# C-weighted sums of a selective scan: two of four sequences moved from VectorE to ScalarE and GpSimd

## What is computed

```python
dt = softplus(ts @ W_dt.T + b_dt)              # 2048 channels
def step(state, inp):                          # over the 128 tokens of a sequence
    dt_t, B_t, C_t, u_t = inp
    dA = exp(dt_t[..., None] * A)              # A: 2048 channels x 16 states
    state = state * dA + (dt_t * u_t)[..., None] * B_t[:, None, :]
    y = einsum('bdn,bn->bd', state, C_t)       # sum over the 16 states, weighted by C
y = (ys + x * D) * silu(gate);  out = y @ W_out.T
```

## Time and profile before

| what | value |
|---|---|
| median of three runs | 3445.48 us |
| span of the profiled execution, first to last instruction | 3444.0 us |
| PE busy | 2894.4 us (84%) |
| DVE busy | 2815.9 us (82%) |
| ACT busy | 1403.2 us (41%) |
| POOL busy | 1399.2 us (41%) |
| first to last `dtu` (15 steps of the scan phase) | 558.7 to 2506.9 us |

### The profile page before, as it was taken

The page is one execution under the profiler, slowest core; times in us unless marked ns, Lnnn a source line. Parts: engine busy times, 40 slices in busy tenths (PEclk is TensorE's granted clock), DMA queues, the critical chain, the costliest instruction groups (busy, mean ns, idle before and its releaser), DMA issues.

```text
span 3444.0 us, 37416 instructions
## 1 busy us (share of the span) xinstructions
PE 2894.4 (84%) x10992; PEld 1521.9 (44%) x10992; DVE 2815.9 (82%) x3919; ACT 1403.2 (41%) x2166; POOL 1399.2 (41%) x455
## 2 busy tenths in 40 slices
PE   7999996877887877887877887877877999999996
PEld 3445453444443434444434444434443455555553
DVE  2333336999999999999999999999998677777775
ACT  1111113534434534534534534534532455555553
POOL 0000004555565565565555665555662122222221
PEclk9999997999999999999999999999999999999998
DMA  4111114120113120113120113120112121111110
GB/s 145 55 55 38 54 49 116 57 110 7 56 62 80 55 104 7 62 50 87 62 100 11 62 50 86 61 89 22 61 37 62 42 75 61 61 61 55 55 61 25
DMA packets 57906, 210.48 MB, mean 61 GB/s; under 512 B 4481, under 2 KB 4609, under 8 KB 52961
## 3 DMA queue, kind: packets, MB, share of 16 engines
q1 hardware_dynamic: 57762, 208.76, 18.2%
HBM read 172.96 MB, written 35.78 MB: 61 GB/s over the span
## 4 chain that ended last, share of the span: by engine, by line
PE 35%; DVE 34%; issue 20%; POOL 4%; ACT 4%; DVEq 2%; DMA 1%; SPq 0%; POOLq 0%; ACTq 0%
DVE arena L662 16%; PE banks L1004 13%; DVE arena L678 10%; PE banks L407 3%; PE banks L450 3%; PE banks L363 2%; PE banks L388 2%; POOL arena L1138 2%; POOL arena L1144 2%; PE banks L418 2%; DVE rbuf L687 2%; PE banks L289 1%; PE banks L378 1%; PE banks L986 1%; DVE arena L745 1%
## 5 line engine op out<-in xcount | busy, mean ns | idle before, releaser
L1144 POOL TENSOR_TENSOR arena<-arena 128x2048 f32<-128x2048 f32 x256 | 1156.9, 4528 | 620.4 <-PE banks L306 618.2
L662 DVE TENSOR_TENSOR_SCAN arena<-banks,arena 128x512 f32<-128x512 f32 x1024 | 1189.3, 1201 | 36.2 <-POOL arena L1144 19.8
L522 ACT ACTIVATE banks<-arena,a_sb 128x508 f32<-128x508 f32 x1024 | 700.1, 687 | 1151.6 <-DVE arena L662 1151.4
L306 PE MATMUL banks<-ident,arena 128*128 128x128 f32 x4096 | 665.2, 292 | 385.5 <-DVE arena L678 350.4
L306 PEld LDWEIGHTS banks<-ident,arena 128*128 128x128 f32 x4096 | 460.7, 146 | 871.7 <-DVE arena L678 712.8
L678 DVE SCALAR_TENSOR_TENSOR arena<-banks,cg,arena 128x512 f32<-128x512 f32 x960 | 664.1, 731 | 1.3 <-PE banks L306 1.0
L289 PE MATMUL banks<-arena 128*128 128x512 f32 x1088 | 523.6, 606 | 5.4 <-issue 5.4
L321 PE MATMUL banks<-arena 128*128 128x512 f32 x1024 | 501.4, 614 | 0.0
L1004 PE MATMUL banks<-arena 128*128 128x512 f32 x1024 | 444.5, 595 | 24.6 <-DMA dsk<-in_D 24.6
L1197 DVE SCALAR_TENSOR_TENSOR arena<-banks,arena 128x508 f32<-128x508 f32 (+2 forms) x192 | 142.6, 742 | 330.8 <-ACT arena L1070 326.3
L1138 POOL TENSOR_TENSOR arena<-arena 128x2048 f32<-128x2048 f32 x16 | 72.4, 4526 | 711.8 <-DMA arena<-u_scratch 551.5
(11 more groups left out here) (131 smaller groups left out, 2481.0 us busy)
## 6 DMA issues: line engine op xcount, KB each, us to landing
arena<-in_WoutT SPq DMA_DIRECT2D x17, 2048.0 KB, 8.0
arena<-in_WinZ SPq DMA_DIRECT2D x64, 512.0 KB, 3.4
arena<-in_xT SPq DMA_DIRECT2D x8, 2048.0 KB, 15.3
u_scratch<-arena SPq DMA_DIRECT2D x16, 1024.0 KB, 5.9
arena<-b_scratch SPq DMA_DIRECT2D x16, 1024.0 KB, 19.9
arena<-u_scratch SPq DMA_DIRECT2D x16, 1024.0 KB, 10.0
arena<-x_scratch SPq DMA_DIRECT2D x32, 512.0 KB, 3.5
x_scratch<-rbuf SPq DMA_DIRECT2D x5, 2048.0 KB, 7.5
```

The lines of the kernel that those rows point to most:

```text
L306: last = nc.tensor.transpose(bank(2 + b % 2)[:, i * P:(i + 1) * P], hb[n % 4][:, i * GT + b * P:i * GT + (b + 1) * P], ident[:, :])
L522: nc.scalar.activation(by_seq(bank(i % 2))[:, :, 1:SEQ], by_seq(dt[q % 2][:, i, :])[:, :, 1:SEQ], ACT.Exp, scale=a_sb[:, QD * q + i, n:n + ...
L662: nc.vector.tensor_tensor_scan(h, bank(i % 2), h, 0.0, ALU.mult, ALU.add)\
L1144: nc.gpsimd.tensor_tensor(hb[n % 4].rearrange("p (i t) -> p i t", i=QD), dtu, brep[:, n:n + 1, :].broadcast_to([P, QD, GT]), ALU.mult)\
```

## The change

VectorE keeps the sums of sequences 0 and 1. For sequences 2 and 3 ScalarE writes C times the turned state into a new tile `part` (one 128x512 slot for each of the two sequences), and GpSimd adds `part` to `acc`. For state 0 ScalarE writes `acc` itself. Bank 2 now serves sequences 0 and 1, bank 3 sequences 2 and 3, and TensorE's turns go in the order 0, 2, filler, 1, 3, filler. To make room for `part` small tiles were moved into the arena, and `ones` is set by GpSimd after the scan phase.

```diff
 def turn(b):
-    pe.wait_ge(S["acc_ok"], 4 * U + b - 1 + ACCD)
+    if b < OWN:
+        pe.wait_ge(S["acc_ok"], OWN * U + b + ACCD)
+    else:
+        pe.wait_ge(S["part_ok"], OWN * U + b - OWN + PARTD)
...
-turn(0); turn(1); filler(0); turn(2); turn(3); filler(1)
+turn(0); turn(2); filler(0); turn(1); turn(3); filler(1)
...
 # before the end-of-step transposes
+pe.wait_ge(S["sum_ok"], OWN * (N - 1) * (s + 1) + SUMD)
...
+def act_part(act, g, q, n, j):
+    s = NQ * g + q
+    b = OWN + j
+    act.wait_ge(S["t_done"], 4 * (N * s + n) + 2 * j + 2 + T_DONE)
+    if n == 0:
+        act.wait_ge(S["yt_mm"], 4 * s + ONE)
+        act.wait_ge(S["cg_ok"], g + 1)
+        dst = acc[:, b, :]
+    else:
+        act.wait_ge(S["sum_ok"], OWN * (N - 1) * s + OWN * n + j - 3 + SUMD)
+        dst = part[:, j, :]
+    nc.scalar.activation(dst, bank(3), ACT.Identity, scale=cg[:, b, n:n + 1])\
+        .then_inc(S["part_ok"], 1)
...
 # act_step, unit n: four exps; act_part(n - 2, 0) before the third, act_part(n - 2, 1) after the fourth
...
+def pool_sums(pool, g, q, n):
+    s = NQ * g + q
+    if n == 0:
+        return
+    for j in range(OWN):
+        done = OWN * (N - 1) * s + OWN * (n - 1) + j
+        pool.wait_ge(S["part_ok"], OWN * (N * s + n) + j + 1 + PARTD)
+        pool.wait_ge(S["sum_ok"], done - 1 + SUMD)
+        v = acc[:, OWN + j, :]
+        nc.gpsimd.tensor_tensor(v, v, part[:, j, :], ALU.add).then_inc(S["sum_ok"], 1)
...
 # pool_step, unit n: the product of n, then
+if n >= 4:
+    pool_sums(pool, g, q, n - 4)
+elif not first:
+    pool_sums(pool, *preceding(g, q), n + N - 4)
...
 # dve_step: one sum, two scans, one sum, two scans
-dve_acc(dve, g, q, n, 2 * part)
-dve_acc(dve, g, q, n, 2 * part + 1)
+dve_acc(dve, g, q, n, part)
```

More of the change, by code:

```diff
@@ L140, in program @@
         bful = at(32544, H)
+        km, nkm, ksum, rk = (at(36864 + OT * i, OT) for i in range(4))
+        qm, qz, qr = (at(36880 + 2 * HEADS * i, 2, HEADS) for i in range(3))
+        ones = at(36992, P)
+        gs, gb, nlm, gsum = (at(36960 + i, 1) for i in range(4))
+        lg, lex, rank, gate = (at(36964 + NE * i, NE) for i in range(4))
+        cgt, cge = (at(36928 + NE * NE * i, NE, NE) for i in range(2))
         rbuf = sb("rbuf", [P, GB, H])
@@ L147, in program @@
         cg = sb("cg", [P, GB, N])
+        part = sb("part", [P, OWN, QD * P])
         dsk = sb("dsk", [P, DT])
@@ L331, in pe_step @@
                 turn(0)
+                turn(2)
+                filler(0)
                 turn(1)
-                filler(0)
-                turn(2)
                 turn(3)
@@ L456, in pe_squares @@
             pe.wait_ge(S["sq_ok"], 2 * b + h + 1)
-            nc.tensor.matmul(bank(5 + 2 * h), ones[:, :], sq[:, h * HALF:(h + 1) * HALF],
+            nc.tensor.matmul(bank(5 + 2 * h), ones, sq[:, h * HALF:(h + 1) * HALF],
                              start=True, stop=True).then_inc(S["ssq_mm"], 1)
@@ L511, in act_softplus, with act_step @@
                 nc.scalar.activation(d, d, ACT.Ln, bias=1.0).then_inc(S["dt_ln"], 1)
-        def act_step(act, g, q, last=False):
+        def act_part(act, g, q, n, j):
[11 more added lines that the diff above has]
+                .then_inc(S["part_ok"], 1)
+        def act_step(act, g, q, first=False, last=False):
             s = NQ * g + q
             for n in range(N):
+                if n >= 2:
+                    before = (g, q, n - 2)
+                else:
+                    before = None if first else (*preceding(g, q), n + N - 2)
                 for i in range(QD):
+                    if i == 2 and before:
+                        act_part(act, *before, 0)
                     e = 4 * (N * s + n) + i
@@ L1090, in _ @@
             act_softplus(act, 0, 0, range(QD))
-            with nc.scalar.Fori(0, NG - 1) as g:
+            for q in range(NQ):
+                act_step(act, 0, q, first=(q == 0))
+            with nc.scalar.Fori(1, NG - 1) as g:
                 for q in range(NQ):
@@ L1095, in _ @@
                 act_step(act, NG - 1, q, last=(q == NQ - 1))
+            for n in (N - 2, N - 1):
+                for j in range(OWN):
+                    act_part(act, NG - 1, NQ - 1, n, j)
             act.wait_ge(S["p2_const"], C2)
@@ L1110, in _ @@
             pool.sem_inc(S["bm_ok"], BM)
[L1111 to L1112 removed]
+            pool.sem_inc(S["dtu_ok"], ONE)
+            pool.sem_inc(S["sum_ok"], SUMD)
             nc.gpsimd.memset(ident[:, :], 0.0)
[L1114 removed]
             nc.gpsimd.memset(mhalf[:, :], -0.5)
```

93 lines of the change are left out of this document (44 added, 49 removed).

## The result

The changed kernel takes 3616.66 us (median of 4 runs, 3612.95 to 3620.00), the kernel before 3448.45 (4 runs, 3442.68 to 3451.78). The ratio is 1.0486, 95% interval [1.0473, 1.0499]: slower by 4.9%. The forecast was 3638.5.

A forecast was written before the change was run, and what follows sets the result against it. VectorE was taken to set the scan phase's pace. To 3444.0 us the forecast added 181.7 between first and last `dtu` and 11.3 after, giving 3637.0, or 3638.5 as median of runs; 8-in-10 range 3530 to 3705.

The forecast's parts named there:

- ordinary step: Scan-phase step away from group edges and without the norm: 140.1 us forecast, against an average of 129.9 before.
- first step: First `dtu` to second in the scan phase: 116.2 us, of which 32.4 to the end of unit 1's first sum.
- norm: Once per group, product 5 waits for the norm's power and its application waits for GpSimd: 10.9 us per group.
- ring: Each unit's loop of turn 3, GpSimd product, sum and ScalarE's copy into the single slot: 7.3 us, against 7.09 before.
- S(1) to S(11): Inside a step, end of GpSimd's first sum of unit 1 to that of unit 11: ten intervals of 7.3 us.
- S(11) to S(12): End of GpSimd's first sum of unit 11 to unit 12's, across dt, the next `dtu` and a product: 19.5 us.
- E to S(1): End of a step's last GpSimd sum to the end of the next step's first sum of unit 1: 22.3 us.
- The wait for dt: At a step's end GpSimd idles about 7 us before the next `dtu`, until VectorE makes dt; VectorE waits next.
- The clock: TensorE's clock drops after idling at a step's end, slowing transposes and filler: 3.2 us per step.
- A cheap ring (1): In the scan units, copy 0.58 us, sum 1.04 and clock staying up: 3534 us, 3500 to 3575; chance 0.12.
- A clock that falls inside units (2): TensorE drops to 1.2 GHz in a sixth of the scan units, 129 us more: 3768 us; chance 0.06.
- That GpSimd sets the pace (3): In the scan phase the copy's wait doesn't bind; GpSimd's throughput does, 119.5 us per step: 3313 us; chance 0.08.

The follow-up runs named there:

- Experiment 1: Changed kernel with two `part` slots per sequence instead of one, GpSimd's order unchanged, B rows of states 14 and 15 replaced to make room: 3443.14 us, ratio 0.9985.
- experiment 2: Changed kernel, one slot, GpSimd doing the sums of unit n-4 before product n and unit 12's before the next step's `dtu`: 3411.33 us, ratio 0.9892.
- Experiment 6: Changed kernel, one slot, only step-end order altered: unit 12's sums before `dtu`, those of 13 to 15 one product earlier: 3514.52 us, ratio 1.0187.
- experiment 7: Changed kernel with only sequence 3's sum moved off VectorE, one slot, GpSimd doing product n before the sum of n-4: 3482.63 us, ratio 1.01.
- experiment 5: Changed kernel with only sequence 3's sum moved, two slots, sum of unit n-4 before product n, unit 12's before `dtu`: 3379.32 us, ratio 0.9794.
- experiment 4: Changed kernel with GpSimd's adds and all waits for them left out, ScalarE still writing the scaled copies: 3231.34 us, ratio 0.9368.

## Why the prediction was right

The direction, the mechanism and its place were as forecast; the time came out 22 us below it, because the ordinary step was forecast too long and the first step and the norm too short. Spans of the profiled execution: forecast 3637.0, measured 3613.0.

| term | forecast | measured |
|---|---|---|
| ordinary step, mean of seven | 140.1 | 136.9 |
| ring, per unit | 7.30 | 7.27 to 7.32 |
| S(1) to S(11) | 75.3 | 74.7 |
| S(11) to S(12) | 19.5 | 18.9 |
| dt ready after S(11) | 8.45 | 8.1 |
| S(12) to S(15) | 21.9 | 22.3 |
| S(15) to E | 1.1 | 1.25 |
| E to S(1) | 22.3 | 20.3 |
| first `dtu` to second | 116.2 | 122.2 |
| norm, per group (mean of four) | 10.9 | 15.3 |
| group's edge (mean of three) | 2.9 | 2.8 |
| last `dtu` to last gate product | 158.0 | 154.9 |

The step's pieces are those of the step that ends at 1142.2: E of the step before at 1004.79, S(1) 1025.05, S(11) 1099.79, S(12) 1118.65, S(15) 1140.94. They sum to 137.4 against the 140.1 forecast. Fourteen steps at 136.9 are 45 us less than forecast. The first step (6.0) and the norm (4 x 4.4 = 18) give 24 back, and the tail takes 3: together the 24 us between the spans. That these errors have opposite signs is luck; each piece is within 0.6 us but for the tail and those named below.

**The ring.** Its sum was right by two errors that cancel. The sum on GpSimd takes 1.27 us, not 1.10 (a quarter of the product was the wrong scale: a product of 2048 takes 4.53), and the copy takes 0.67, not 0.78. The lines' durations (ns min/median/max):

```profile
L659 POOL TENSOR_TENSOR arena<-arena,part x480: 1249/1267/1732, 595.6 to 2815.6; 128x512 f32<-128x512 f32 x160
...
L522 ACT ACTIVATE part<-banks,cg x480: 664/674/692, 588.4 to 2814.8; 128x512 f32<-128x512 f32 x160
```

With 4.53 + 1.25 (half of a pair) + 0.67 + 0.66 the handovers have 0.16 to 0.21 left, 0.24 in the forecast. That the circle is the cause, and not an engine, is shown by experiments 1 and 2, which open it in two different ways and both arrive at 6.93 to 6.95.

**The wait for dt** was right in size (7.15 us idle, about 7 forecast) and in what it holds. Experiment 6 shows its price, 102 us with one slot; experiment 7 against 5 gives 103, with the second slot taken away as well. Experiment 1 shows that a second slot removes it without touching the order.

**The clock** was the largest term too high, 2.0 of the step's 3.2. After E TensorE has been idle 5.44 us. The granted clock is 0.50 (the level of 1.2 GHz) from 1004 to 1010 and 1.00 (2.4 GHz) from 1010.2 to 1014, 0.69 over these ten us:

```profile
1004.92 4.02 PE L349 MATMUL banks<-ident,arena 128*128 128x128 f32 x16 [5.44 <-POOL arena L659]
...
1010.30 1.88 PE L317 MATMUL banks<-arena 128*128 128x512 f32 x4
```

The transposes are slow (4.02 us for 16, as the 1.97 for 8 in the earlier trace rows), but the filler behind them already runs at full clock: 1.88 us, where the forecast had put 3.2. I had laid the low clock over the filler as well, by the earlier trace rows. The piece took 20.3 us: 0.6 above its reckoning at full clock (19.7), where I had put 2.6.

**The first step** was too low by 6.0 us, 5.2 of which lie before S(1): it came at 596.8, 37.6 after `dtu`, not 32.4. The product of unit 5, which waits for the turns of unit 1, starts at 591.05. The scans were as forecast (9.03 us from 568.33); behind them stands VectorE's copy of C:

```profile
577.28 4.48 DVE L767 COPY cg<-cbt 128x64 f32 x1
...
581.79 0.75 DVE L729 TENSOR_SCALAR arena<-banks,cg 128x512 f32<-128x512 f32 x1
```

VectorE's first sum of state 0 waits for it, and the turns wait for that sum. The prediction had this copy before it, 4.48 us at 577.0 in the earlier trace rows, and used it for the norm but put nothing for it in the first step: that is 4.5 of the 5.2 us. TensorE, idle 5.0 us meanwhile, then worked at a granted clock of 0.51 from 580 to 587 (its filler took 3.15 us); the last 0.7 fit that but were not measured by themselves.

**The norm** was too low by 4.4 per group. In the first one the waiting part (E to S(1)) took 30.35 us, forecast 30.8, but against an ordinary 20.3 that adds 10.1, not 8.5. The rest is the application, which the forecast had at 2.4 us beside GpSimd. VectorE's timeline:

```profile
757.34 6.85 DVE L761 TENSOR_SCALAR rbuf<-rbuf,mv,ve 128x1024 f32<-128x1024 f32 x4
```

It took 6.85 us instead of 3.05, and the products around it are 11.9 us apart (755.06, 766.97) instead of 7.3. The prediction had the mechanism, a wait for the GpSimd instruction beside it, but charged it once; it is paid by three of the four parts (last section).

**Rivals.** A cheap ring (1) fell: a copy with a scale column costs 0.67, but the dearer sum takes that back. Its other half, that the clock stays up, was near the truth for the filler. A clock that falls inside units (2) fell: 0.97 from 1040 to 1090. That GpSimd sets the pace (3) is what the kernel would do without its circle and with the sums out of dt's way, as experiment 2 shows, but at 6.95 us a unit. The forecast of 3313 for it was 98 too low. Its step of 119.5 took 124.5: GpSimd is busy 113.4 us of it instead of 109.5, since a sum takes 1.25 and not 1.10, and idle 11.1 instead of 10. The norm took 14.8 instead of 8.5. 15 x 5.0 + 4 x 6.3 is 100.

## What to carry to other kernels

When work is split over engines through a buffer with one slot, write the circle down (who releases whom, until the first name returns) and add its durations before comparing busy shares: here a circle of 7.3 us beat 7.09 of a full VectorE, with GpSimd, the fullest engine, at 6.95. Then look where on each engine's fixed list the new instruction stands: a cheap sum behind a wait for something unrelated (dt) cost 102 us of the 168. It costs only where the producer has no other slot: an order that puts consumers first got the whole loss back with one slot (3411 us), and a second slot got it back with the old order (3443). A smaller share moved, in that order, was the best version (0.9794 [0.9777, 0.9812]).

## What the runs showed of the hardware

Two kinds of VectorE instruction, the norm's scale (128x1024, SBUF to SBUF) and the gate product (128x512, both inputs in SBUF), wait for the GpSimd instruction that is running when they start: they end 0.55 us after it, however long it takes. The norm's application in the changed kernel, then in experiment 4, where GpSimd makes no sums (durations ns min/median/max; 16 of the 20 lie in the scan phase):

```profile
L761 DVE TENSOR_SCALAR rbuf<-rbuf,mv,ve x20: 800/1746/2908, 757.3 to 2904.7; 128x1024 f32<-128x1024 f32 x20
```
```profile
L759 DVE TENSOR_SCALAR rbuf<-rbuf,mv,ve x20: 799/802/3454, 725.4 to 2522.1; 128x1024 f32<-128x1024 f32 x20
```

The median is 1.75 us in the first and 0.80 in the second, as in the kernel before. In experiment 4 it is the first of each group's four that is long (2.26 to 3.45 us), each started in a product. In all nine traces together 92 of these scales started beside a running GpSimd instruction, and every one ended 0.55 to 0.56 us after it; the other 88 took about 0.80. GpSimd pays as well: beside the four scales in the rows of the norm, its two sums take 3.38 us, 1.71 each instead of 1.25.

```profile
759.55 3.38 POOL L659 TENSOR_TENSOR arena<-arena,part 128x512 f32<-128x512 f32 x2
```

The gate product shows the same. In experiment 5 it took 2.24 us beside a GpSimd product and 0.68 a moment later (VectorE's timeline):

```profile
1077.37 2.24 DVE L807 TENSOR_TENSOR arena<-arena 128x512 f32<-128x512 f32 x1
...
1080.18 0.68 DVE L807 TENSOR_TENSOR arena<-arena 128x512 f32<-128x512 f32 x1
```

It happened once per step, 15 times in each of experiments 2, 5 and 6, whose orders let a GpSimd product run there; each of the 45 ended 0.55 us after that product. In the other six traces GpSimd is idle there and all take 0.68 to 0.70. And the first copy of C, 128x64, which takes 0.2 us elsewhere, starts 0.1 us behind the fourth product in all nine traces and ends 0.06 us after it, 4.48 us later.

The sums and scans of VectorE, which read one operand from PSUM, keep their mean lengths beside the same work (731 and 734 ns for the sums, 1201 and 1207 for the scans, before and after). What exactly the two engines share there no run of this case shows. And an add of 128x512 costs GpSimd 1.27 us, where a product with a broadcast operand of the same shape costs 1.04; which of the two differences (the operation or the broadcast) makes the 0.23 was not tried.
